# A stack of local attention: VectorE divides the outputs of the unit ahead before it takes the score maxima

## The reference, cut to what matters

```
q, k, v = split(shift_tokens(x) @ Wqkv)             # 16 heads of 64
q, k = l2norm(q) * qs, l2norm(k) * ks, then rotary tables (cos, sin, scale)
sim  = 8 * einsum('bhwie,bhwje->bhwij', q_window, k_window_and_the_one_before)   # 32 x 64
attn = softmax(where(mask, -max, sim), -1)
out  = einsum('bhwij,bhwje->bhwie', attn, v_windows)
x    = out @ Wo + x
x    = (a * gelu(gate)) @ W2 + b2 + x    # layernorm(shift_tokens(x)) @ W1 + b1 = a, gate
```

## Time and profile before

| what | value |
|---|---|
| median of three runs | 4236.03 us |
| profiled execution | 4233.4 us, its span 4231.6 us |
| PE busy | 3830.4 us (91%) |
| POOL busy | 3038.0 us (72%) |
| DVE busy | 2736.0 us (65%) |
| ACT busy | 2673.6 us (63%) |
| granted TensorE clock, mean | 0.964 |

### The profile page before, as it was taken

One profiled execution on the slowest core, in us unless ns is written; L12 is line 12 of the kernel. 1 busy time (PEld: TensorE's weight loads), 2 busy tenths in 40 slices (PEclk: granted clock), 3 DMA queues, 4 the chain that ended last, 5 costly groups with the idle time before them and its releaser, 6 DMA issues.

```text
span 4231.6 us, 164819 instructions
## 1 busy us (share of the span) xinstructions
PE 3830.4 (91%) x69412; PEld 2711.6 (64%) x69412; DVE 2736.0 (65%) x5013; ACT 2673.6 (63%) x5570; POOL 3038.0 (72%) x1908
## 2 busy tenths in 40 slices
PE   7989999999999999977999999999999999447986
PEld 5556676676676666654676667666667666235655
DVE  5566676676677776644676677777667676553762
ACT  6657676676767676654666767666666766224762
POOL 1088888888888888833988888888888888433003
PEclk9999999999999999999999999999999999758988
DMA  2033443433334343321334344343443433012004
GB/s 93 2 84 93 105 104 96 108 100 104 102 94 115 96 109 101 92 70 32 96 96 112 91 110 103 94 113 98 107 103 90 113 96 92 1 48 86 2 8 136
DMA packets 342894, 369.52 MB, mean 87 GB/s; under 512 B 58769, under 2 KB 277906, under 8 KB 341842
## 3 DMA queue, kind: packets, MB, share of 16 engines
q1 hardware_dynamic: 339218, 352.91, 32.2%
q0 software_dynamic: 2944, 6.10, 0.4%
HBM read 250.98 MB, written 111.86 MB: 86 GB/s over the span
## 4 chain that ended last, share of the span: by engine, by line
PE 76%; DVE 8%; ACT 6%; issue 6%; POOL 3%; DMA 1%; SPq 0%; DVEq 0%; POOLq 0%; ACTq 0%
PE banks L338 13%; PE banks L366 8%; PE banks L379 8%; PE banks L426 7%; PE banks L467 6%; PE banks L322 5%; PE banks L306 4%; PE banks L411 4%; PE banks L396 3%; PE banks L461 3%; ACT arena L1070 2%; DVE arena L626 2%; PE banks L297 2%; PE banks L1000 1%; PE banks L1463 1%
## 5 line engine op out<-in xcount | busy, mean ns | idle before, releaser
L696 POOL TENSOR_TENSOR arena<-arena 128x512 f32<-128x512 f32 x768 | 959.8, 1271 | 370.9 <-DVE arena L626 235.5
L701 POOL TENSOR_TENSOR arena<-arena 128x1024 f32<-128x1024 f32 x384 | 905.9, 2359 | 30.1
L698 POOL TENSOR_TENSOR arena<-arena 128x1024 f32<-128x1024 f32 x384 | 908.1, 2365 | 0.0
L626 DVE SCALAR_TENSOR_TENSOR arena<-arena,banks 128x512 f32<-128x512 f32 x768 | 493.6, 684 | 509.2 <-ACT arena L509 502.3
L338 PE MATMUL banks<-w_qk,arena 128*128 128x512 f32 x1536 | 734.6, 601 | 16.4 <-DVE arena L801 10.6
L477 ACT COPY arena<-banks 128x512 f32<-128x512 f32 x384 | 224.1, 584 | 612.4 <-PE banks L426 611.9
L619 DVE TENSOR_REDUCE arena<-arena 128x8 f32<-128x512 f32 x768 | 487.3, 670 | 79.3 <-ACT arena L493 73.2
L493 ACT ACTIVATE arena<-banks 128x512 f32<-128x512 f32 x768 | 441.0, 593 | 64.4 <-PE banks L338 49.9
L338 PEld LDWEIGHTS banks<-w_qk,arena 128*128 128x128 f32 x1536 | 276.7, 193 | 271.9 <-issue 271.9
L426 PE MATMUL banks<-ident,arena 128*128 128x128 f32 x3072 | 424.4, 281 | 26.5 <-POOL arena L701 20.6
L379 PE MATMUL banks<-w_v,arena 128*128 128x256 f32 x1536 | 395.0, 380 | 0.0
(11 more groups left out here) (244 smaller groups left out, 6509.8 us busy)
## 6 DMA issues: line engine op xcount, KB each, us to landing
v_rows<-arena SPq DMA_DIRECT2D x1536, 64.0 KB
arena<-v_rows SPq DMA_DIRECT2D x768, 128.0 KB
arena<-v_rows SPq DMA_DIRECT2D x768, 112.0 KB
arena<-in_moe_w SPq DMA_DIRECT2D x30, 515.5 KB, 3.4
w_qk<-in_stack_qk SPq DMA_DIRECT2D x48, 256.0 KB, 3.1
w_v<-in_stack_v SPq DMA_DIRECT2D x48, 128.0 KB, 3.3
w_o<-in_stack_o SPq DMA_DIRECT2D x12, 512.0 KB
w_w<-in_stack_w SPq DMA_DIRECT2D x12, 341.0 KB, 3.2
```

Source lines behind the costliest of these rows:

```text
L626: last = nc.vector.scalar_tensor_tensor(qn[:, :, tile], rn, 1e12, bank(M, tile).rearrange("p (h q d) -> p h q d", h=GH, q=2), ALU.min, ALU ...
L696: nc.gpsimd.tensor_tensor(f.sined[:, :, :, half, :], x[:, :, :, 1 - half, :], sines[:, :, mine].unsqueeze(1).to_broadcast([D, GH, 4, DH // ...
L698: nc.gpsimd.tensor_tensor(rot, x.rearrange("p h t a d -> p h t (a d)"), cosines.unsqueeze(1).to_broadcast([D, GH, 4, DH]), ALU.mult).then_ ...
L701: nc.gpsimd.tensor_tensor(rot, rot, f.sined.rearrange("p h t a d -> p h t (a d)"), ALU.add).then_inc(S.rotated, 1)
```

## The change

In `dve_stack_step` the block with lag 4 (the division) moves in front of the first block with lag 3 (maxima and differences). No instruction, wait or increment is added or taken away; the second block with lag 3 (row sums, reciprocal) stays where it is.

```diff
     dve_stack_hidden(M, st, 0)
+    if st.on(4):
+        u = s - 4
+        st.wait(S.outs, u + 1)
+        st.wait(S.inverted, u + 1)
+        st.wait(S.outs_turned, u)
+        nc.vector.tensor_tensor(f.o.rearrange("p (x b) d -> p x b d", b=2), two_banks(M, T, DH),
+                                f.inv.rearrange("p (x b) -> p x b", b=2).unsqueeze(3).to_broadcast([D, 4, 2, DH]),
+                                ALU.mult).then_inc(S.normed, 1)
     if st.on(3):
         u = s - 3
         sv = two_banks(M, 0, KW)
@@
         nc.vector.tensor_tensor(f.zs.rearrange("p (x b) k -> p x b k", b=2), sv,
                                 top.unsqueeze(3).to_broadcast([D, 4, 2, KW]), ALU.subtract).then_inc(S.shifted, 1)
-    if st.on(4):
-        u = s - 4
-        st.wait(S.outs, u + 1)
-        st.wait(S.inverted, u + 1)
-        st.wait(S.outs_turned, u)
-        nc.vector.tensor_tensor(f.o.rearrange("p (x b) d -> p x b d", b=2), two_banks(M, T, DH),
-                                f.inv.rearrange("p (x b) -> p x b", b=2).unsqueeze(3).to_broadcast([D, 4, 2, DH]),
-                                ALU.mult).then_inc(S.normed, 1)
     if st.on(3):
```

## The result

| kernel | median us | runs |
|---|---|---|
| before | 4234.03 (4229.18 to 4236.15) | 4 |
| changed | 4288.14 (4280.45 to 4289.0) | 4 |

The ratio is 1.0129, 95% interval 1.0117 to 1.0142: 54 us slower, where 46 were forecast (4282 against 4288). The profiled execution took 4289.0 us, its span 4287.2 us against 4231.6, 55.6 us more.

The account below looks back on a forecast made before the run. TensorE was taken to bound the kernel, nearly every stall in the stacks being paid. Losses of 24 + 19 + 3 = 46 us on the profiled 4233.4 gave 4279, so 4282 us for the median; range 4252 to 4312.

Parts of the forecast that it names:

- The gain: TensorE's waits at L396 for the division, at most 10.0 us; in step 3 its 0.22 us are spent waiting at L411.
- the faster rival: Step 3: if ScalarE reaches L541 before TensorE wants it, the 10.0 us come back; 4226 us, chance 0.06.
- Step 4 into 5: Later exponential and token copies delay TensorE's mean, L411 and L442 by 0.52 us in 46 pairs: 24 us loss.
- Step 3: Later exponential delays ScalarE's L541, so TensorE's L366 comes 0.41 us later in 46 pairs: 19 us loss, L396 gain included.
- Step 7: Later L541 delays the load of L366; 0.06 us taken for the matmul, 48 times: 3 us loss.
- Where it costs nothing: Steps 0 to 2, 5 and 6: slack before TensorE or GpSimd takes up the later exponential; no loss.
- the leak rival: Covers in steps 5, 6 and 1 too thin: 0.3 us in two steps more of 46 pairs, 28 us; 4310, chance 0.17.
- The chances: Whole kernel: slower by over 0.2% 0.88, same 0.06, faster 0.06; the forecast itself (4266 to 4296 us) 0.60.
- What would show it: Changed profile: L396's wait gone, L366 waiting 0.2 to 0.4 us, L438 stalled about 0.5, pair 67.6 us instead of 66.6.
- The two signs of being wrong: L366 shows no wait, or the wait before L438 is there but that before L442 shrinks by it.

## Why the prediction came out right, step by step

**The gain is 10 us and is spent.** Spent, yes: L396 does not wait in step 3, and L411 behind it waits 0.45 us for the exponential. Its size was wrong. The prediction took the idle time as the cost of the wait and had L396 go on at 915.58, 0.22 us earlier; it starts 0.38 us earlier in the changed kernel (4.19 us after the start of step 3 in place of 4.57), and the wait closed without the exchange gave 18 us, not 10. As the gain is spent in this kernel, the sum did not feel it; the price of the faster rival (4226) would have.

**Step 4 into 5, 24 us.** Right in the chain: 0.50 us in place of 0.52. That it came so near is in part luck, for small slips in the working cancel. The copies end 0.50 us later in the median, not 0.58, because the division starts 0.07 us sooner after the same `outs` than the maxima did (1.65 and 1.72 us after the start of the step). The mean starts 0.15 us after the copies, not 0.05, and L411 follows it 0.94 us later, not 0.97. The 0.15 us stood between copies and mean before too, and the mean moved by just what the copies moved, so TensorE was waiting there already, only not shown as idle. The claim that L442 adds nothing held (0.74 us before and after).

**Step 3, 19 us.** Right: 0.42 against 0.41 us. The profile has the working's cause: L541 comes 0.60 us later and L366's load 0.52, as forecast. The 0.41 was the middle of a range for the first matmul; that matmul comes only 0.31 us later, but its group takes 3.72 us in place of 3.62, so the near match is in part luck. L411's wait uses up the gain and 0.17 us more (5.24 in place of 5.07 us after the start of the step).

**Step 7, 3 us.** Nearly nothing: in the pair shown the load of L366 came 0.05 us after L541, as at a wait, and in 11 of 46 pairs it did wait, 2.1 us in all; the step did not grow.

**Where it costs nothing.** This is the step that failed: the prediction put the other steps at nothing, and they cost 12 to 14 us in the full change (54 or 55.6 less 42), 17 alone. The forecast missed by 8 only because it had 4 us for steps 4 and 7 that did not come. No cover in step 5 gave way and step 6 grew by 0.03 us in the median, so the leak rival failed in its mechanism; its price, 28 us, was twice too high. For step 1 the prediction followed the exponential to L411 and the scaling to GpSimd; VectorE's product L658, which also stands behind the row sums, and TensorE's wait for it are not in it. The matmul L467 itself had slack enough, 0.29 us being left of 0.89, and that slack would not have told of the cost: the exchange in step 1 alone takes 9 us, by longer stops in step 2. The rest of the remainder lies in other steps and is open but for a few us of stops in step 1.

**The chances.** The faster rival rested on ScalarE reaching L541 in time. It does not: the load of L366 stands 0.33 us for it. The Trainium skill's rule weighed in the prediction (Perfetto Trace Analysis, "Optimization Strategy") named the right gap. Closing it by moving L663, for which no instruction on TensorE's path had to stand back, gave 18 us; closing it by the exchange cost 19 in that step alone.

**What would show it.** The pair was to be 67.6 us long (66.6 + 1.0); the medians of the eight steps add up to 66.7 before and 67.6 after. From pair to pair, the stops included, the median length is 67.7 and 68.9 us. The forecast that ScalarE's idle time before the exponential would grow by 0.6 us in two steps and by hundredths elsewhere was wrong, it stood idle in 371 of 384, for a median 0.33 to 0.94 us in the steps other than 1 and 3; most of those steps just did not lie on TensorE's path. The two signs of being wrong did not show: L366's load waits in step 3, and L442's wait did not shrink.

## What to carry to other kernels

When two independent operations of an in-order engine are exchanged, price the one that steps back before the one that steps forward, and with it everything queued behind it: here the differences feed a softmax, a ScalarE queue without holes and two TensorE waits, the division only one. An operation that stood between a producer and its own later consumer on the same engine was filling a wait; see what could fill it instead. A slack read at an instruction's start can miss what a later wait costs the instructions queued behind it, and the idle time shown before a waiting matmul can be less than the wait costs (0.22 shown, 0.38 paid). And a visible wait may cover a second one just behind it, so look one step further before counting it as a gain.

## What was not expected of the hardware

TensorE's stops in the middle of 64 short matmuls, with no semaphore between, total 41 to 65 us over the twelve experiments and two kernels. Those of step 2 fall in the same 18 pairs of 48 or fewer of them. A shift of 0.6 us later or 1.0 us earlier of one VectorE operation, at a wait that itself shows no idle time, took the stops of step 2 from 13.1 to 21.7 or to 7.0 us. The single stop shown above went from 0.41 to 1.71 us, more than the shift ahead of it, while the mean of them grew by 0.50; why single ones differ so is open.
